# Mamba pairs: growth factors as rows in HBM, spread by one transfer per pair

## What is computed

```python
cum = jnp.cumsum(dA, axis=2)
decay = jnp.exp(jnp.where(mask[None, None, :, :, None], diff, -jnp.inf))
Y_diag = jnp.einsum('bcijh,bcjhp->bcihp', scores, x_c)
states = jnp.einsum('bclh,bclhn,bclhp->bchpn', decay_states * dt_c, B_c, x_c)
_, prev_states = lax.scan(step, init, (jnp.moveaxis(states, 1, 0), jnp.moveaxis(chunk_decay, 1, 0)))
state_decay_out = jnp.exp(cum)
Y_off = jnp.einsum('bclhn,bchpn,bclh->bclhp', C_c, prev_states, state_decay_out)
hidden = yr * jax.nn.silu(gate)
```

## Time and profile before

| | us |
|---|---|
| median of 3 runs | 2031.29 (2029.26 to 2031.56) |
| the profiled execution, its time | 2029.76 |
| its span, first to last instruction | 2028.0 |
| PE busy | 1951.2 |
| DVE busy | 1457.5 |
| ACT busy | 1302.5 |
| POOL busy | 834.3 |
| `growth` on ACT, 128 instructions | 106.8 |

### The profile page before, as it was taken

One profiled execution on the slowest core, in us unless ns is written; L12 is line 12 of the kernel. 1 busy time (PEld: TensorE's weight loads), 2 busy tenths in 40 slices (PEclk: granted clock), 3 DMA queues, 4 the chain that ended last, 5 costly groups with the idle time before them and its releaser, 6 DMA issues.

```text
span 2028.0 us, 43010 instructions
## 1 busy us (share of the span) xinstructions
PE 1951.2 (96%) x12684; PEld 1588.1 (78%) x12684; DVE 1457.5 (72%) x2600; ACT 1302.5 (64%) x2978; POOL 834.3 (41%) x1000
## 2 busy tenths in 40 slices
PE   5999999999999999999989999999999999999998
PEld 4888678888788857888878885788878888588886
DVE  4775468888677457888857745788886773588886
ACT  3664269999555237888835523788884551488885
POOL 2120158888300005777620001577771000177776
PEclk8999999999999999999989999999999999999999
DMA  5330236566222113444412201344442220144442
GB/s 201 117 116 24 91 120 206 197 204 210 94 83 74 41 41 121 153 150 153 151 60 89 79 25 44 130 151 152 150 143 76 79 73 21 48 161 150 152 149 79
DMA packets 119115, 231.00 MB, mean 114 GB/s; under 512 B 10448, under 2 KB 48528, under 8 KB 118928
## 3 DMA queue, kind: packets, MB, share of 16 engines
q1 hardware_dynamic: 119056, 230.26, 34.5%
HBM read 194.05 MB, written 36.18 MB: 114 GB/s over the span
## 4 chain that ended last, share of the span: by engine, by line
PE 64%; issue 22%; ACT 9%; DVE 2%; POOL 2%; ACTq 1%; DMA 0%; POOLq 0%; DVEq 0%
PE bank L655 26%; PE bank L894 9%; PE bank L881 5%; PE bank L870 4%; PE bank L861 3%; PE bank L783 2%; PE both L655 2%; PE bank L775 2%; PE bank L755 2%; PE both L775 2%; PE bank L853 2%; ACT span_b L1158 2%; ACT place L1158 2%; ACT shared L1164 1%; PE bank L797 1%
## 5 line engine op out<-in xcount | busy, mean ns | idle before, releaser
L655 PE MATMUL bank<-xn_r,w_r 128*128 128x512 f32 x2304 | 631.6, 414 | 18.0 <-DVE place L1457 7.2
L655 PEld LDWEIGHTS bank<-xn_r,w_r 128*128 128x128 f32 x2304 | 425.1, 191 | 128.6 <-issue 41.9
L1315 DVE SCALAR_TENSOR_TENSOR conv_acc<-bank,conv_sb,conv_acc 128x511 f32<-128x511 f32 (+2 forms) x408 | 304.3, 746 | 51.0 <-ACT conv_acc L1076 17.3
L534 POOL TENSOR_TENSOR rstd<-var_eps,minus_half 128x4 f32<-128x4 f32 (+2 forms) x12 | 9.7, 809 | 664.0 <-DVE var_eps L1262 664.0
L1012 ACT ACTIVATE place_r<-bank 128x512 fp32r<-128x512 f32 (+1 forms) x320 | 158.1, 556 | 156.6 <-PE bank L655 128.7
L894 PE MATMUL bank<-wo_n,place 128*128 128x256 f32 x1024 | 255.1, 392 | 1.6 <-DVE place L1440 1.6
L1249 DVE TENSOR_TENSOR place_r<-bank,place_r 128x512 fp32r<-128x512 f32 (+1 forms) x320 | 186.7, 632 | 87.7 <-ACT place_r L1012 87.7
L555 POOL TENSOR_TENSOR shared<-shared,c_t 128x768 f32<-128x768 f32 x128 | 234.5, 1832 | 0.0
L894 PEld LDWEIGHTS bank<-wo_n,place 128*128 128x128 f32 x1024 | 184.0, 189 | 42.9 <-issue 21.2
L577 POOL TENSOR_TENSOR sumsq<-sumsq,place 128x512 f32<-128x512 f32 x128 | 163.5, 1277 | 110.6 <-ACT place L1065 110.6
L655 PE MATMUL bank<-place_r 128*128 128x512 f32 (+3 forms) x960 | 193.7, 342 | 9.4 <-DVE place_r L1249 6.8
(11 more groups left out here) (154 smaller groups left out, 3497.6 us busy)
## 6 DMA issues: line engine op xcount, KB each, us to landing
place_r<-cum_rows SPq DMA_DIRECT2D x128, 512.0 KB, 3.8
w_r<-pair_split SPq DMA_DIRECT2D x96, 512.0 KB, 3.7
w_r<-qkv_split SPq DMA_DIRECT2D x48, 512.0 KB, 4.0
pair_split<-w_r SPq DMA_DIRECT2D x32, 512.0 KB, 4.0
qkv_split<-w_r SPq DMA_DIRECT2D x16, 768.0 KB, 3.8
w_r<-qkv_split SPq DMA_DIRECT2D x48, 256.0 KB, 3.2
wo_n<-out_split SPq DMA_DIRECT2D x96, 128.0 KB, 3.5
raw<-in_w_pair SPq DMA_DIRECT2D x32, 256.0 KB, 3.8
```

Of the source, the lines that this page charges most:

```text
L655: ins = mm(out, lhsT=w(a), rhs=m(b), start=(start and i == 0), stop=(stop and i == 2), **kw)
L1315: stt(out=conv_acc[:, back:W], in0=src[:, 0:W - back], scalar=conv_sb[:, ch, TAPS - 1 - back:TAPS - back], in1=conv_acc[:, back:W], op0=AL ...
```

## The change

Growth factors are computed once per sequence: ACT takes the exponential of `neg_cum` with scale -1, 64 heads by 512 tokens on the partitions, into the tile `square`, before the first `spans`. SP stores these 64 rows in HBM as `grow_rows` and waits for the landing. For each pair, a new `grow_load` copies its two rows, without the first chunk, to all 128 partitions into `c_grow`, 384 KB; `weigh_c` on POOL waits for that landing. `growth` goes from ACT. `spread_load` now waits on the count of `s_span`. `grow_load(n)` waits until `off_block(n-2)` has read the buffer (`s_off_done`), for the first two pairs until the FFN's last matmuls (`s_ffn_out`), since `c_grow` shares its memory with the FFN's hidden tile. The first `squares` of a sequence waits until the rows are stored.

```diff
+            def grow_save(b):
+                sp.wait_ge(s_grow_ev, b + 1)
+                sp.dma_start(grow_rows[bass.ds(b, 1), :, :].rearrange("b h w -> h (b w)"), square[0:MH, :]).then_inc(s_grow_saved, 16)
+                sp.wait_ge(s_grow_saved, b * 16 + 16)
+
+            def grow_load(b, n, par):
+
+                if isinstance(n, int) and n < 2:
+                    sp.wait_ge(s_ffn_out, b + 1)
+                else:
+                    sp.wait_ge(s_off_done, b * NPAIR + n)
+                sp.dma_start(c_grow[:, par, :, :], grow_rows[bass.ds(b, 1), bass.ds(n * 2, 2), P:W]
+                             .to_broadcast([P, 2, W - P])).then_inc(grow_in[par], 16)
...
                 else:
-                    sp.wait_ge(s_grow_ev, b * NPAIR + n - 1)
+                    sp.wait_ge(s_span, b * NPAIR + n - 1)
...
                 with sp.Fori(1, NPAIR // 2 - 1) as i:
                     for par in range(2):
+                        grow_load(0, i * 2 + par, par)
                         pair_save(i * 2 + par, par)
                         pair_load(i * 2 + par + 2, par)
...
+                grow_save(b)
+                for n in range(2):
+                    grow_load(b, n, n)
                 with sp.Fori(0, NPAIR // 2 - 1) as i:
                     for par in range(2):
                         sp.wait_ge(s_w_used, b * NPAIR + i * 2 + par + 1)
                         pair_fetch(i * 2 + par + 2, par)
                         spread_load(b, i * 2 + par + 2, par)
                         out_fetch(b, i * 2 + par, par)
+                        grow_load(b, i * 2 + par + 2, par)
...
             def weigh_c(b, n, par):
-                pool.wait_ge(s_grow_ev, b * NPAIR + n + 1)
+                pool.wait_ge(grow_in[par], (b * NPAIR + n - par + 2) * 8)
...
-                def growth(n, par):
-
-                    A(c_grow[:, par, :, :], spread[:, par, :].rearrange("p (h w) -> p h w", h=2)[:, :, P:W], ACT.Exp,
-                      scale=-1.0).then_inc(s_grow_ev, 1)
...
                 act.wait_ge(s_cum_t_ready, b + 1)
+                act.wait_ge(s_summed, b * (NPAIR + 1) + NPAIR + 1 - NPAIR)
+                A(square, neg_cum, ACT.Exp, scale=-1.0).then_inc(s_grow_ev, 1)
                 spans(0, 0)
                 act.wait_ge(s_ffn_out, b + 1)
-                growth(0, 0)
                 mixes(0, 0)
...
                         conv_tanh(K + n + 3, bank[2])
-                        growth(n + 1, 1 - par)
```

More of the change, by code:

```diff
@@ L238, in two_layers @@
         s_grow_ev = sem("grow_ev")
+        s_grow_saved = sem("grow_saved")
+        s_grow_in0 = sem("grow_in0")
+        s_grow_in1 = sem("grow_in1")
+        grow_in = (s_grow_in0, s_grow_in1)
         s_off_done = sem("off_done")
@@ L298, in two_layers @@
         pair_split = nc.dram_tensor("pair_split", [NPAIR, P, 2, 2 * D], F32, kind="Internal").ap()
+        grow_rows = nc.dram_tensor("grow_rows", [NB, MH, W], F32, kind="Internal").ap()
         cum_rows = nc.dram_tensor("cum_rows", [NB, MH, W], F32, kind="Internal").ap()
@@ L441, in first_sequence @@
                     spread_load(0, n, n)
+                grow_save(0)
                 for n in range(2):
@@ L445, in first_sequence @@
                     spread_load(0, n + 2, n)
+                    grow_load(0, n, n)
                     out_load(n, n)
@@ L454, in first_sequence @@
                 for par in range(2):
+                    grow_load(0, NPAIR - 2 + par, par)
                     pair_save(NPAIR - 2 + par, par)
@@ L1064, in squares @@
                 act.wait_ge(s_summed, N + b + 1)
+                if isinstance(n, int) and n == 0:
+                    act.wait_ge(s_grow_saved, b * 16 + 16)
                 A(square, hid, ACT.Square).then_inc(s_squared, 1)
```

## The result

| | before | after |
|---|---|---|
| median, us | 2030.28 (4 runs; 2031.29 stood ahead) | 2114.82 (2113.52 to 2121.88, 4 runs) |
| ratio, 95% interval | | 1.0415 (1.0398 to 1.0432) |
| span of the profiled execution, us | 2028.0 | 2113.7 |

The change is slower by 84.5 us. I had forecast +18.6 and a range to 2075: the sign was right, the size wrong by a factor of 4.5.

The account below looks back on a forecast made before the run. PE (TensorE) was taken to bound all 128 pairs. Late weight fetches cost +19.1 us, the last sequence's start gains 0.5: 2031.29 + 18.6 = 2050 us, 0.9% slower, range 2029 to 2075.

Parts of the forecast that it names:

- The bound: All 128 pairs: PE sets the pace at 7.82 us a pair, so taking growth from ACT gives back nothing.
- The third rival: First sequence's 30 steady pairs: ACT is the bound, up to 0.84 us a pair returns, 2025 us; chance of faster 0.05.
- What leaves ACT: Growth exponentials, 106.8 us in all: nothing gained in the loops, 0.5 us once at the last sequence's start.
- The first sequence: SP's order there is growth load, `pair_save`, `pair_load`; data land in time by 1 us, cost nothing.
- The mechanism in the later sequences: Sequences 1 to 3: growth load's wait for `off_block` delays the weight fetch; PE late 0.22 us a pair, 19.1 us.
- the count of 87: Weight fetches delayed: those of pairs 3 to 31, 29 a sequence, in three sequences.
- the third of the list: Landing of the weight fetch behind the growth load: 3.7 + 0.75 x 0.6 = 4.15 us after its issue.
- The second rival: Four transfers issued within 2.5 us disturb each other: landing 4.6 us, stall 0.67 a pair, 2089 us; chance 0.16.
- break-even of 0.23 us: Slack of PE's projection a pair if the weights land in 3.7 us: early by 0.23, so no stall.

Follow-up runs that it names:

- the last run above: Changed kernel, but in sequences 1 to 3 the next pair's growth load, with its wait, stands behind the early weight fetch: 2031.59 us, ratio 0.9999.
- the run with 64 KB: Changed kernel, growth load in the loop of sequences 1 to 3 cut from 384 KB to 64 KB in 128 pieces, other factors stale: 2058.65 us, ratio 1.0129.
- nothing behind: Changed kernel, but SP waits for the weights' landing before issuing cumulative rows and output weights; growth load stays ahead: 2099.83 us, ratio 1.0338.
- long pieces: Changed kernel, growth rows stored without their first chunk, so the 384 KB load has 128 pieces instead of 256: 2102.3 us, ratio 1.0349.
- the tiny load: Changed kernel, growth load in the loop of sequences 1 to 3 cut to 8 KB in 16 pieces, other factors stale: 2037.32 us, ratio 1.0026.
- the weights first: Changed kernel, but after the same wait for `off_block` SP issues the weight fetch first and the growth load behind it: 2035.84 us, ratio 1.0018.
- the wait alone: Kernel before the change, with only a wait for `off_block` added ahead of the weight fetch in sequences 1 to 3: 2034.61 us, ratio 1.0011.

## Why the prediction was wrong in size

**The bound, right.** PE sets the pace in all sequences. ACT's relief changed no pair in the first sequence (7.81 to 7.82) and none in the last run above. The third rival, ACT as the bound, is refuted. The growth rows came in time everywhere: no engine's row shows a wait for them.

**What leaves ACT, right.** At the start of the last sequence PE waited 1.49 us for DVE's first product before and 0.89 after: 0.6 gained where I said 0.5.

```profile
1770.91 1.61 PE L655 MATMUL bank<-xn_r,w_r 128*128 128x512 f32 x6 [1.49 <-DVE place L1457]
...
1833.84 1.62 PE L682 MATMUL bank<-xn_r,w_r 128*128 128x512 f32 x6 [0.89 <-DVE place L1481]
```

**The first sequence, right.** I had the growth load issued at 305.96, `pair_load` at 307.5 and landed at 312.3, with the DMA share at 0.77. The trace has 305.89, 307.32 and 311.97, and the share is 0.78. A wait of the same kind costs nothing there, because what stands behind it isn't late.

```profile
305.89 0.39 SPq L433 DMA_DIRECT2D shared<-grow_rows  x1
306.54 0.58 SPq L391 DMA_DIRECT2D pair_split<-w_r  x1
307.32 0.45 SPq L378 DMA_DIRECT2D raw<-in_w_pair  x1
```

**The mechanism in the later sequences, right**, and so was the count of 87. The terms from one `off_block`'s end to the next, after the change as means of the 28 steady turns of each of the three loops:

| term, us | predicted | after |
|---|---|---|
| SP reacts | 0.18 | 0.18 |
| growth load's issue to the weights' issue | 0.73 | 0.80 |
| weights' issue to landing | 4.15 | 4.75 |
| landing to PE | 0.12 | 0.14 |
| projection, turn, `off_block` | 2.86 | 2.89 |
| sum | 8.04 | 8.77 |

The loop closes: the mean length of these turns is 8.77 us too (the terms are rounded). It is 0.73 more than predicted, 63 us over 87 turns, and 0.60 of that, 52 us, is the landing. With their own landing and spacing, and 0.18 + 0.14 + 2.89 = 3.22 for the rest, three other runs come out as well: 3.22 + 0.75 + 4.14 = 8.11 in the run with 64 KB (8.10 measured over the same turns), 3.22 + 0.80 + 4.49 = 8.51 with nothing behind (8.54), 3.22 + 0.75 + 4.57 = 8.54 with long pieces (8.57). With the tiny load the sum is 3.22 + 0.75 + 3.76 = 7.73 and the pair 7.85: there the loop doesn't close through the transfer in every turn.

**The step that failed is the third of the list, the landing.** I took the slowing from one pair of rows, and scaled it by the size of the transfer ahead: 0.6 us for 512 KB, hence 0.45 for 384. Measured is 1.05. Three things were wrong in it. First, of the three places in the trace of before where one weight fetch follows another, 0.6 us behind it, I had shown the fastest, 4.3 us; the others are 4.4 and 5.2, and I set 5.2 aside as a single case. The same code stands unchanged in all nine traces of this case, and the second fetch lands there after 4.3 to 5.4 us, 4.8 in the mean of 27. With 4.8 the same scaling gives a landing of 4.5 and an estimate of 52 us in place of 19, still short. Second, the scaling itself: 384 KB in 256 pieces ahead make the weights land as late, 4.75, as 512 KB in 256 pieces do, 4.8; the long pieces show that the number of pieces counts beside the bytes. Third, I read from the same rows that what comes behind does no harm, since the first of the two took only 3.6. The run with nothing behind shows 0.25 us of harm where the growth load is ahead. The second rival, a burst of four that disturb each other, with a landing of 4.6 for 2089 us and a chance of 0.16, came nearest with its number. Its mechanism holds for that quarter of a microsecond alone: with the weights first the same four move in the same burst, and the weights land in 3.7.

**The spacing on SP has a second side.** The growth load's own issue took 0.38 us, not the 0.55 of the fetches with as many pieces, but every second turn goes through the loop's branch, and the next issue comes 1.00 us behind it instead of 0.65 (825.00 to 826.00 in the chain above). Over the three loops these are 0.98 and 0.63 us. The turn with the longer spacing isn't the longer one: its weights land after 4.40 us, those issued 0.63 behind the growth load after 5.09, and so the turn through the branch takes 8.60 us and the other 8.94. The two turns of the chain show it with 4.29 and 5.17. With nothing ahead the two turns differ as well, but less: 3.77 and 3.99 us with the wait alone, 3.65 and 3.90 with the weights first. So what is left, 0.4 to 0.5 us, goes with the spacing, as far as these runs show; none changed the spacing alone. A price by size can't give it.

The other errors are small: 0.02 us at the wake after a landing, 0.03 at the projection and its followers. But the stall is a difference of large numbers: at a break-even of 0.23 us each tenth of a microsecond is worth 8.7 us over 87 pairs. So the range should have been far wider: a landing between the 3.7 and the 5.2 of the earlier trace rows is 0 to 110 us, and I cut that to 45.

The Trainium skill ("DMA: Bandwidth & Descriptors", section "Anatomy of one DMA") gives a fit for one transfer issued by GpSimd, 2.0 us plus the bytes by 436 GB/s; for transfers issued by SP, as all are here, it gives none. Carried over to the growth rows and the weights together it would be an estimate of 2.0 + 2.1 us after the first issue. The trace doesn't agree: the mean is 0.80 + 4.75 = 5.55 us. The advice of the Trainium skill (the same page, section "Rules for kernel authors") to issue early and wait late is what the last experiment does, and the trace agrees: 10.4 us from issue to use, and no stall.

**The last sequence, 0.2 us a pair shorter, is accounted for.** SP's issues are 0.75 us apart there, not 0.82, and PE starts 0.04 us after a landing, not 0.19; together that is the 0.22 us between the pairs. The last sequence's chain:

```profile
1901.70 4.65 DMA w_r<-pair_split
1906.34 0.04 issue
1906.39 1.66 PE bank L682 x6
```

The last sequence's program stands outside the loop over the sequences; that this is the reason was not tried.

**What stays open.** Of the 1.05 us some 0.25 go with what is behind and 0.19 with half of the pieces ahead (the two may overlap). How the rest divides between bytes and pieces is not shown, nor where in the transfer engines the time passes. The growth load also reads the same two rows for all 128 partitions; a load of as many bytes and pieces from rows of their own was not tried.

## What to carry to other kernels

In a queue that issues in order, a wait delays all that stands behind it, so a new transfer with a later wait belongs behind the urgent one: here the swap of two transfers was worth 79 us, and with the right place the time was that of the kernel before. Where a forecast rests on a slack of a few tenths of a microsecond between a transfer's landing and its use, don't price the landing by its median alone: take its spread when others are in flight, and multiply by the number of turns before setting the range. When only a few rows show how transfers delay each other, look for every place with the same two transfers in all traces at hand. And taking work from an engine that is 98% busy gained nothing here, where the loop was as long with that engine 86% busy.

## What the runs showed of the hardware

A transfer's landing depended on its neighbours in the same queue, and more on those ahead than behind. A fetch of 512 KB landed in 3.7 us alone or behind 8 KB, in 4.2 behind 64 KB, in 4.6 behind 384 KB in 128 pieces, in 4.7 behind 384 KB in 256 pieces (medians), in 4.8 behind another 512 KB (the mean of 27), and in 3.7 again with those 384 KB and 640 KB more right behind it. Issued 0.63 us behind the growth load it landed in 5.09 us, issued 0.98 behind in 4.40; with nothing ahead the same two turns differed by 0.2 to 0.25. Between the growth load's issue and the next on SP lay 0.65 us or 1.00 us in the second sequence, by whether the loop's branch stands between them. PE started 0.19 us after a landing in the second and third sequences, and 0.04 in the last.
